# Second layer of a graph network: the running count of the placing scan moves into a PSUM bank, and its multiplication goes ahead of the next scan

## Chip, cores and metric

The kernel runs on one core of a Trainium2 chip (trn2). The metric is device time in microseconds (us) of one execution; the time of the kernel before is the median of three runs.

## What is computed

Two layers of a graph network over 12500 nodes of 128 channels and 400000 edges that are sorted by `dst`. The first is an attention layer over the edges. The second, which the change touches, is a weighted sum of neighbours, a linear layer and a normalization:

```python
x = _layernorm(x + _L0_gnn_ref(x, node_vec, edge_weight, edge_attr_64, edge_index, ...))
# second layer: rows = src, cols = dst, vals = edge_weight
gathered = vals[:, None] * x[cols]
agg = jax.ops.segment_sum(gathered, rows, num_segments=N_NODES)
x = _layernorm(x + jnp.einsum('nc,oc->no', agg, W) + b)
```

The edges are sorted by `dst`, but the second layer sums by `src`. So each edge's message must first be brought to a place beside the other messages of its target.

## The kernel before

**Blocks and steps.** The nodes are cut into 98 blocks of 128 (NB = 98). The second layer takes the edges in 808 steps of four tiles of 128 edges (G = 4, so 512 edges a step), in unrolled rounds of eight steps; in a round `st.k` runs from 0 to 7 and `st.i` counts the rounds. All engines run through the same steps, each with its stages at fixed leads: `(count_stage, 9)` in a step means that the count of the step nine ahead is done there. Each engine issues its stages in the order in which `body1` lists them, and semaphores tie the stages together.

**How an edge finds its place.** SyncE loads for each edge the number of its `src` block (`blk_row`, to 98 partitions). On VectorE `in_blk_stage` (L1751) compares it with the partition's number and so makes `in_blk`, 98 x 512 values of 0 or 1 in bf16, two buffers. `count_stage` (L1769) runs a scan along the 512 edges, state times one plus membership, so that each block's partition holds its running count; the scan starts from the last element of the former step's scan, or, in the first step of a round, from `carry`, which `carry_stage` (L1757) makes of that element and a jump from a table. The ones are read from bank 7 (`one_ps`). The scan writes `ranks`, which are the two halves of `y_all` in SBUF, taken in turn. `found_stage` (L1776) multiplies the ranks by the membership into one of four buffers `found1`, so that each edge keeps only the count of its own block. TensorE sums these over the partitions with a vector of ones (`rank_stage`, L1045), and VectorE copies the result to the table (`posw_stage`, L1783).

**The message.** VectorE makes a one-hot of the edges' `dst` (`onehot1_stage`, L1794), TensorE gathers with it the rows of the node matrix (L1063), ScalarE scales them into a ring of four steps (`rows_out`, L1261 and L1262) and takes the table rows (`take1`, L1254); VectorE forms the offsets (`rel_stage`, L1788) and the final index (`pick_stage`, L1801, and `place_stage`, L1808). GpSimd then issues four indirect scatters a step to DRAM (L869), after it has waited for the rows and for the index.

**Segments.** From round 26 of 101 on, a second stream runs in the same loop: SyncE loads messages back in their new order (three segments a step), VectorE makes their one-hots (`seg_rels`, L1821, and `seg_onehots`, L1828), TensorE multiplies (L1077), and VectorE adds the three products to the sums in SBUF (`seg_add`, L1838), each add waiting for the one before. After the pairs' last step the segments run alone, and the closing normalization follows.

**The waits around the change.** A scan waits for `s_inblk`, for `s_pos` up to the multiplication of the step two before it (two places), and for `s_carry`, which counts scans and carries. The multiplication waits for `s_carry` and for the rank matmul that last read its output buffer. `s_pos` counts the multiplications. Bank 0 is unused in this part of the kernel.

Of the kernel before, what the change touches and what calls it, by code (L numbers as in the profile page):

```python
# [19 lines left out]
ALU = mybir.AluOpType  # L20
# [3 lines left out]
P = 128  # L24
G = 4
# [24 lines left out]
def build(nc, x, src, dst, attr, weight, node_vec, time_w, time_b, Wq, bq, Wk, bk, Wv, bv, We, Wskip, bskip, W1, b1, out):  # L50
# [5 lines left out]
    NB = -(-N // P)  # L56
# [30 lines left out]
    with ctx:  # L87
        def sb(name, shape, dt=F32):
            return ctx.enter_context(nc.sbuf_tensor(name, shape, dt))

        def sem(name):
            return ctx.enter_context(nc.semaphore(name))
# [32 lines left out]
        jump = sb("jump", [P, NCHUNKS])  # L125
        carry = sb("carry", [P, 1])
# [56 lines left out]
        prod = y_all[:, :].rearrange("p (k e) -> p k e", k=2)  # L183
# [29 lines left out]
        def part(n):  # L213

            rest1[0] += n
            return kv_flat[:, rest1[0] - n:rest1[0]]
# [4 lines left out]
        in_blk = part(G * P).bitcast(BF16).rearrange("p (k e) -> p k e", k=2)  # L221
# [12 lines left out]
        seg_oh = oh_all[:, RING1 * G * P:RING1 * G * P + SEG_OH * SEGMENT * 2 * P].rearrange("p (h b a n) -> p h b a n", h=SEG_OH, b=SEGMENT, a=2)  # L234
        assert MT == 4 * SEGMENT and UNROLL1 % (MT // SEGMENT) == 0
        blk_row = feat_flat[:, RING1 * 2 * P:RING1 * 2 * P + KS * G * P // 2].bitcast(BF16).rearrange("p (k e) -> p k e", k=KS)
        ranks = prod
        found1 = [featT_all[:, 0, :], featT_all[:, 1, :], feat_flat[:, 0:G * P], feat_flat[:, G * P:2 * G * P]]
        zeros = oh_all[:, QS * G * P * 2 - (CHUNK * NCHUNKS - COLS) * 4:QS * G * P * 2]
        W7 = FB * C  # L240
# [32 lines left out]
        def hist(n, of):  # L273
# [26 lines left out]
        banks = [ctx.enter_context(nc.psum_tensor(f"bank{i}", [P, 512], F32)) for i in range(8)]  # L300
# [2 lines left out]
        featT_ps = banks[1][0:TD + MSG, :]  # L303
        e_ps, q_ps = banks[2:4], banks[4:6]
        agg_ps = [banks[6 + j][:, 0:HEADS * HB] for j in range(2)]
        irow_ps, one_ps = banks[7][:, 0:P], banks[7][0:NB, P:P + 1]
        RANKS = SEGMENT * P
        mT_ps, small_ps = banks[0][:, 0:G * ROWS], banks[0][:, 128:128 + 4 * ROWS]
# [35 lines left out]
        s_chunk, s_carry, s_inblk, s_rank, s_pos, s_posw = (sem(n) for n in (  # L344
            "s_chunk", "s_carry", "s_inblk", "s_rank", "s_pos", "s_posw"))
# [17 lines left out]
        def wait(eng, s, value):  # L363

            if not isinstance(value, int) or value > 0:
                eng.wait_ge(s, value)
# [26 lines left out]
        def Step1(i, k):  # L393
            return Step(i, k, UNROLL1)

        def exists(st, steps):
            return not isinstance(st.s, int) or 0 <= st.s < steps
# [54 lines left out]
        def at1(i, k, *stages):  # L452

            for stage_of, ahead in stages:
                st = Step1(i, k + ahead)
                if exists(st, STEPS1):
                    stage_of(st)

        def seg(i, k, b, ahead, pairs, stage_of):
            st = Step1(i, k + ahead)  # L460
            first, end = (BEGIN, LOOPS1) if pairs else (LOOPS1, ENDS)
            if not isinstance(st.s, int) or UNROLL1 * first <= st.s < UNROLL1 * end:
                stage_of(Segment(st, b))
# [829 lines left out]
        def _(dve):  # L1293
# [459 lines left out]
            def carry_stage(st):  # L1753

                if st.k == 0 and not (isinstance(st.i, int) and st.i == 0):
                    dve.wait_ge(s_carry, st.s + st.i - 1)
                    dve.tensor_tensor(carry[0:NB, :], ranks[0:NB, 1, G * P - 1:G * P], jump[0:NB, bass.ds(st.i, 1)], ALU.add).then_inc(s_carry, 1)  # L1757

            def count_stage(st):

                dve.wait_ge(s_inblk, st.s + 1)
                wait(dve, s_pos, st.before(2))
                first = isinstance(st.i, int) and st.i == 0
                if st.k == 0:
                    since = jump[0:NB, 0:1] if first else carry[0:NB, :]
                else:
                    since = ranks[0:NB, (st.k + 1) % 2, G * P - 1:G * P]
                wait(dve, s_carry, st.s + st.i)
                dve.tensor_tensor_scan(ranks[0:NB, st.k % 2, :], one_ps.to_broadcast([NB, G * P]), in_blk[0:NB, st.k % 2, :], since,  # L1769
                                       ALU.mult, ALU.add).then_inc(s_carry, 1)  # L1770

            def found_stage(st):

                dve.wait_ge(s_carry, st.s + st.i + 1)
                wait(dve, s_rank, st.before(4))
                dve.tensor_tensor(found1[st.k % 4][0:NB, :], ranks[0:NB, st.k % 2, :], in_blk[0:NB, st.k % 2, :], ALU.mult).then_inc(s_pos, 1)  # L1776

            def posw_stage(st):

# [32 lines left out]
            def seg_blocks(i, k):  # L1812
                sg = Segment(Step1(i, k), 0)
                seg_blk[k] = several(mybir.EngineType.DVE, seg_blk_i[0:1, bass.ds(sg.q, SEGMENT)], NB)
# [25 lines left out]
            def body1(i, pairs, segs):  # L1840
                for k in range(UNROLL1):
                    own = segs and (not isinstance(i, int) or i >= (BEGIN if pairs else LOOPS1))
                    if segs:
                        seg(i, k, 0, 2, pairs, seg_onehots)
                    if own:
                        seg_blocks(i, k)
                    if pairs:
                        at1(i, k, (onehot1_stage, 2), (carry_stage, 9), (count_stage, 9))
                    if segs:
                        seg(i, k, 0, 0, pairs, seg_add)  # L1850
                    if pairs:
                        at1(i, k, (posw_stage, 6), (place_stage, 0), (found_stage, 8))
                    if segs:
                        seg(i, k, 1, 0, pairs, seg_add)
                    if pairs:
                        at1(i, k, (rel_stage, 4), (in_blk_stage, 10))
                    if segs:
                        seg(i, k, 2, 0, pairs, seg_add)
                    if pairs:
                        at1(i, k, (pick_stage, 1))  # L1860
                    if segs:
                        seg(i, k, 0, 3, pairs, seg_rels)
# [13 lines left out]
            dve.wait_ge(s_base1, 1)  # L1876
            dve.wait_ge(s_acc1, 1)
            second(dve, body1)

            def products(g, i, k):  # L1880
# [63 lines left out]
```

## Time and profile before

| | |
|---|---|
| median of 3 runs | 9850.37 us (9843.33 to 9854.15) |
| the profiled execution | 9864.48 us |
| its span in the trace | 9862.8 us |
| VectorE busy | 8560.3 us (87%) |
| TensorE busy | 7624.6 us (77%) |
| GpSimd busy | 6708.6 us (68%) |
| ScalarE busy | 5115.0 us (52%) |
| TensorE's granted clock, mean | 0.822 |

The span is the time from the first to the last instruction of the profiled execution. DVE is VectorE, ACT is ScalarE, POOL is GpSimd, PE is TensorE and PEld its weight load, SP is SyncE. A busy share is an average over both layers; the second layer's pairs lie between 5225 and 9449 us. In a row of the timeline the number in brackets is the time for which the engine was idle ahead of the instruction, with what ended it.

### The profile page before, as it was taken

The numbers are of one execution on the slowest core, as the hardware profiler recorded it, in microseconds if no ns is written. First come the engines' busy times: TensorE is split into PE (matmuls) and PEld (weight loads), VectorE is DVE, ScalarE is ACT, GpSimd is POOL, SyncE is SP. The second block draws the span as 40 slices with busy tenths as digits, with TensorE's granted clock in tenths as the row PEclk, the third lists the DMA queues.
The fourth block names the chain that finished last, engine by engine and source line by source line (L and its number), as shares of the span: only waits on it lengthen the run. The fifth ranks groups of instructions, "written<-read, shape, count | busy, mean of one in ns | idle before, by whom it ended". The sixth has DMA issues, their size and how long they took to land.

```text
span 9862.8 us, 272152 instructions
## 1 busy us (share of the span) xinstructions
PE 7624.6 (77%) x52868; PEld 7101.3 (72%) x52869; DVE 8560.3 (87%) x21301; ACT 5115.0 (52%) x20838; POOL 6708.6 (68%) x6871
## 2 busy tenths in 40 slices
PE   6477777777777777777756777788888888888855
PEld 2477777777777777777756777787888877877754
DVE  5899999999999999999987666799999999999968
ACT  2377777777777777777753333333333333333300
POOL 0477777777777777777745777777777777777720
PEclk8688988888888888898875555688888888888888
DMA  6467666676666666666632222355555555555544
GB/s 191 114 180 178 179 177 177 178 179 178 176 177 180 177 176 177 178 181 177 177 97 69 71 71 71 106 151 147 149 147 149 148 148 149 148 148 149 148 133 116
DMA packets 1631706, 1484.67 MB, mean 151 GB/s; under 512 B 792007, under 2 KB 1363043, under 8 KB 1631203
## 3 DMA queue, kind: packets, MB, share of 16 engines
q1 hardware_dynamic: 1374244, 848.34, 34.3%
q0 software_dynamic: 257088, 632.95, 22.8%
q14 instruction: 335, 2.74, 0.1%
q8 instruction: 39, 0.64, 0.0%
HBM read 1225.51 MB, written 254.87 MB: 150 GB/s over the span
## 4 chain that ended last, share of the span: by engine, by line
issue 25%; DVE 19%; POOL 18%; PE 14%; DMA 7%; ACT 7%; DVEq 6%; SPq 3%; ACTq 2%; POOLq 0%
POOL message_scratch L869 17%; DMA message_scratch<-ohT,idx 6%; PE bank L982 3%; DVE y_all L1537 3%; PE bank L973 3%; ACT arena L1154 2%; DVEq L531 2%; PE bank L955 2%; PE bank L1015 2%; PE bank L963 2%; DVE acc L1670 1%; SPq L728 1%; DVE oh L1583 1%; DVE oh L1576 1%; DVE kve L1523 1%
## 5 line engine op out<-in xcount | busy, mean ns | idle before, releaser
L817 POOL DMA_INDIRECT kv<-kv_scratch,arena x3136 | 3265.7, 1041 | 1236.6 <-issue 837.5
L869 POOL DMA_INDIRECT message_scratch<-ohT,idx x3232 | 3214.2, 994 | 1079.0 <-issue 880.2
L1261 ACT ACTIVATE ohT<-bank,kv 128x128 f32<-128x128 f32 x3232 | 923.9, 369 | 2703.8 <-DMA message_scratch<-ohT,idx 2665.1
L1154 ACT ACTIVATE arena<-arena,weights 128x65 f32<-128x65 f32 x7040 | 1771.6, 337 | 2.4 <-PE bank L982 2.3
L1063 PE MATMUL bank<-acc,oh 128*128 x6464 | 1211.2, 345 | 520.3 <-ACT ohT L1262 514.4
L1063 PEld LDWEIGHTS bank<-acc,oh 128*128 128x128 f32 x6464 | 1054.7, 247 | 627.7 <-issue 625.2
L1077 PE MATMUL bank<-oh,kve 128*128 128x128 f32 x8640 | 1387.7, 321 | 144.7 <-DVE arena L1838 107.8
L982 PE MATMUL bank<-arena,oh 128*128 128x130 f32 x7040 | 1164.1, 318 | 280.8 <-DVE acc L1670 274.8
L1077 PEld LDWEIGHTS bank<-oh,kve 128*128 128x128 f32 x8640 | 1248.0, 227 | 167.8 <-issue 157.3
L982 PEld LDWEIGHTS bank<-arena,oh 128*128 128x128 f32 x7040 | 1048.2, 227 | 362.6 <-issue 295.1
L973 PE MATMUL bank<-arena,ohT 128*128 128x128 f32 x7040 | 1090.6, 306 | 0.0
L973 PEld LDWEIGHTS bank<-arena,ohT 128*128 128x128 f32 x7040 | 1031.3, 225 | 0.3 <-issue 0.2
L1161 ACT ACTIVATE featT<-bank 96x512 f32<-96x512 f32 x880 | 518.3, 589 | 917.0 <-PE bank L955 895.0
L963 PE MATMUL bank<-We,featT 96*128 96x128 f32 x7040 | 979.5, 284 | 18.3 <-ACT featT L1161 18.3
L963 PEld LDWEIGHTS bank<-We,featT 96*128 96x128 f32 x7040 | 914.3, 202 | 21.4 <-ACT featT L1161 20.1
L1178 ACT ACTIVATE feat<-wrow,rel 128x32 f32<-128x32 f32 x3520 | 830.6, 308 | 163.7 <-POOL rel L825 161.2
L1769 DVE TENSOR_TENSOR_SCAN y_all<-bank,y_all,kv 98x512 f32<-98x512 f32 x707 | 900.4, 1274 | 0.2
L955 PE MATMUL bank<-ident,feat 128*96 128x128 f32 x3520 | 610.7, 301 | 311.9 <-ACT feat L1167 297.5
L1828 DVE TENSOR_TENSOR oh<-bank,kv 128x768 f32<-128x768 f32 x720 | 689.5, 958 | 76.3 <-DVE kv L1821 37.5
L1518 DVE TENSOR_TENSOR arena<-kv,bank 128x512 f32<-128x512 f32 x880 | 597.9, 679 | 159.2 <-PE bank L963 103.6
L1045 PEld LDWEIGHTS bank<-ones,featT 98*128 98x128 f32 x3232 | 516.9, 242 | 226.6 <-issue 173.5
L1794 DVE TENSOR_SCALAR oh<-bank,icol 128x512 f32<-128x512 f32 x808 | 605.5, 749 | 74.5 <-issue 35.5
(232 smaller groups left out, 12653.6 us busy)
## 6 DMA issues: line engine op xcount, KB each, us to landing
kve<-message_scratch SPq DMA_DIRECT2D x2160, 129.0 KB
kve<-nodes_scratch SPq DMA_DIRECT2D x880, 256.0 KB
feat<-in_edge_attr_dram SPq DMA_DIRECT2D x880, 96.0 KB
feat<-block_scratch SPq DMA_DIRECT2D x812, 98.0 KB
arena<-q_scratch SPq DMA_DIRECT2D x880, 64.0 KB
message_scratch<-ohT,idx POOLq DMA_INDIRECT x3232
kv<-kv_scratch,arena POOLq DMA_INDIRECT x3136
feat<-in_edge_attr_dram SPq DMA_DIRECT2D x880, 32.0 KB
```

The lines of the kernel that those rows point to most:

```text
L817: pool.indirect_dma_start(kv[:, k, g, :], None, kv_d, bass.IndirectOffsetOnAxis(ap=group_rows[:, half, k * G + g, 0:1].bitcast(I32), axis= ...
L869: pool.indirect_dma_start(msg_d, bass.IndirectOffsetOnAxis(ap=idx[:, k, g:g + 1], axis=0), sum_ring[:, k % RING1, g, :], None).then_inc(s_ ...
L955: op = pe.transpose(featT_ps[:, g * P:(g + 1) * P], feat[:, k, g, :], ident[:, :])
L963: op = pe.matmul(e_ps[st.k % 2][:, g * P:(g + 1) * P], featT[:, st.k % 2, g * P:(g + 1) * P], We1[:, :], start=True, stop=True)
L973: op = pe.matmul(q_ps[st.k % 2][:, g * P:(g + 1) * P], ohT[:, r, g * P:(g + 1) * P], qb[:, r, :], start=True, stop=True)
L982: op = pe.matmul(agg_ps[st.k % 2], oh[:, st.k % QS, g, :], wv[:, st.k % 2, g, :, :].rearrange("p h c -> p (h c)"), start=(g == 0), stop=(g ...
L1063: op = pe.matmul(banks[2 + st.k % 2][:, g * P:(g + 1) * P], oht1[:, st.k % RING1, g * P:(g + 1) * P], acc[:, bass.ds(places[g], C)], start ...
L1077: op = pe.matmul(banks[4 + sg.half][:, b * P:(b + 1) * P], mt[:, sg.slot(MT) + b, a, 0:C], seg_oh[:, sg.half, b, a, :], start=(a == 0), st ...
L1154: op = act.activation(wv[:, st.k % 2, g, h, :], vR[:, st.k, g, h, :], ACT.Copy, scale=weights[:, st.k // ROUND, g, st.k % ROUND, h:h + 1])
L1178: op = act.activation(feat[:, k, g, 0:TD], wrow[:, :], ACT.Copy, scale=of[:, g:g + 1])
L1261: act.activation(sum_ring[:, st.k % RING1, g, 0:C], banks[2 + st.k % 2][:, g * P:(g + 1) * P], ACT.Copy, scale=taken[:, st.k, g, 2:3])
L1769: dve.tensor_tensor_scan(ranks[0:NB, st.k % 2, :], one_ps.to_broadcast([NB, G * P]), in_blk[0:NB, st.k % 2, :], since, ALU.mult, ALU.add). ...
```

## The change

`ranks` becomes one place of 98 x 512 values, all of bank 0 in PSUM, in place of the two halves of `y_all` in SBUF. The scan writes it there, and the multiplication, the carry and the next scan's start value read it there. As there is one place, a scan now waits for the multiplication of the step right before it (`wait(dve, s_pos, st.s)`). The multiplication's stage is moved: in a step of the loop it stood behind `place_stage`, between the first and the second add; now it stands behind `onehot1_stage` and ahead of the carry and the scan. Its lead of eight steps stays, and so do all other stages.

```diff
--- before.py
+++ after.py
@@ -234,7 +234,6 @@
         seg_oh = oh_all[:, RING1 * G * P:RING1 * G * P + SEG_OH * SEGMENT * 2 * P].rearrange("p (h b a n) -> p h b a n", h=SEG_OH, b=SEGMENT, a=2)
         assert MT == 4 * SEGMENT and UNROLL1 % (MT // SEGMENT) == 0
         blk_row = feat_flat[:, RING1 * 2 * P:RING1 * 2 * P + KS * G * P // 2].bitcast(BF16).rearrange("p (k e) -> p k e", k=KS)
-        ranks = prod
         found1 = [featT_all[:, 0, :], featT_all[:, 1, :], feat_flat[:, 0:G * P], feat_flat[:, G * P:2 * G * P]]
         zeros = oh_all[:, QS * G * P * 2 - (CHUNK * NCHUNKS - COLS) * 4:QS * G * P * 2]
         W7 = FB * C
@@ -303,6 +302,7 @@
         featT_ps = banks[1][0:TD + MSG, :]
         e_ps, q_ps = banks[2:4], banks[4:6]
         agg_ps = [banks[6 + j][:, 0:HEADS * HB] for j in range(2)]
+        ranks = banks[0][0:NB, :]
         irow_ps, one_ps = banks[7][:, 0:P], banks[7][0:NB, P:P + 1]
         RANKS = SEGMENT * P
         mT_ps, small_ps = banks[0][:, 0:G * ROWS], banks[0][:, 128:128 + 4 * ROWS]
@@ -1754,26 +1754,26 @@
 
                 if st.k == 0 and not (isinstance(st.i, int) and st.i == 0):
                     dve.wait_ge(s_carry, st.s + st.i - 1)
-                    dve.tensor_tensor(carry[0:NB, :], ranks[0:NB, 1, G * P - 1:G * P], jump[0:NB, bass.ds(st.i, 1)], ALU.add).then_inc(s_carry, 1)
+                    dve.tensor_tensor(carry[0:NB, :], ranks[:, G * P - 1:G * P], jump[0:NB, bass.ds(st.i, 1)], ALU.add).then_inc(s_carry, 1)
 
             def count_stage(st):
 
                 dve.wait_ge(s_inblk, st.s + 1)
-                wait(dve, s_pos, st.before(2))
+                wait(dve, s_pos, st.s)
                 first = isinstance(st.i, int) and st.i == 0
                 if st.k == 0:
                     since = jump[0:NB, 0:1] if first else carry[0:NB, :]
                 else:
-                    since = ranks[0:NB, (st.k + 1) % 2, G * P - 1:G * P]
+                    since = ranks[:, G * P - 1:G * P]
                 wait(dve, s_carry, st.s + st.i)
-                dve.tensor_tensor_scan(ranks[0:NB, st.k % 2, :], one_ps.to_broadcast([NB, G * P]), in_blk[0:NB, st.k % 2, :], since,
+                dve.tensor_tensor_scan(ranks, one_ps.to_broadcast([NB, G * P]), in_blk[0:NB, st.k % 2, :], since,
                                        ALU.mult, ALU.add).then_inc(s_carry, 1)
 
             def found_stage(st):
 
                 dve.wait_ge(s_carry, st.s + st.i + 1)
                 wait(dve, s_rank, st.before(4))
-                dve.tensor_tensor(found1[st.k % 4][0:NB, :], ranks[0:NB, st.k % 2, :], in_blk[0:NB, st.k % 2, :], ALU.mult).then_inc(s_pos, 1)
+                dve.tensor_tensor(found1[st.k % 4][0:NB, :], ranks, in_blk[0:NB, st.k % 2, :], ALU.mult).then_inc(s_pos, 1)
 
             def posw_stage(st):
 
@@ -1845,11 +1845,11 @@
                     if own:
                         seg_blocks(i, k)
                     if pairs:
-                        at1(i, k, (onehot1_stage, 2), (carry_stage, 9), (count_stage, 9))
+                        at1(i, k, (onehot1_stage, 2), (found_stage, 8), (carry_stage, 9), (count_stage, 9))
                     if segs:
                         seg(i, k, 0, 0, pairs, seg_add)
                     if pairs:
-                        at1(i, k, (posw_stage, 6), (place_stage, 0), (found_stage, 8))
+                        at1(i, k, (posw_stage, 6), (place_stage, 0))
                     if segs:
                         seg(i, k, 1, 0, pairs, seg_add)
                     if pairs:
```

## Rows read from the trace of the kernel before

**Rows 1.** The page, busy time of each engine over the span

```profile
PE 7624.6 (77%) x52868; PEld 7101.3 (72%) x52869; DVE 8560.3 (87%) x21301; ACT 5115.0 (52%) x20838; POOL 6708.6 (68%) x6871
```

**Rows 2.** The scatter's line: durations (min/median/max), releasers of its idle time

```profile
L869 POOL DMA_INDIRECT message_scratch<-ohT,idx x3232: 955/962/1526, 5250.1 to 9447.8; - x191
...
  issue: 880.2, 2889
```

**Rows 3.** Windows of the second layer: start:end, length, busy time (count), clock, DMA

```profile
5250.10:6339.70 1089.60, 847.33 (x4292) 795.94 (x4290) 677.12 (x1742) 381.36 (x2100) 836.15 (x832) 0.51 0.26 75
6339.70:9448.70 3109.00, 2602.40 (x18981) 2457.81 (x18980) 2846.64 (x7780) 1095.98 (x5947) 2378.04 (x2400) 0.85 0.55 147
...
9383.00:9449.00 66.00, 26.27 (x191) 24.07 (x190) 22.85 (x75) 15.91 (x77) 50.09 (x52) 0.74 0.26 77
```

**Rows 4.** Timeline, VectorE and GpSimd: start, us, instruction, [idle before]

```profile
5252.87 0.97 POOL L869 DMA_INDIRECT message_scratch<-ohT,idx  x1 [0.30 <-ACT ohT L1262]
...
8002.06 1.27 DVE L1769 TENSOR_TENSOR_SCAN y_all<-bank,y_all,kv 98x512 f32<-98x512 f32 x1
8002.18 0.97 POOL L869 DMA_INDIRECT message_scratch<-ohT,idx  x1 [0.30 <-issue]
...
8003.25 0.26 DVE L1838 TENSOR_TENSOR arena<-arena,bank 128x128 f32 x1
...
8003.50 0.15 DVE L1808 TENSOR_TENSOR idx<-kv 128x4 int32<-128x4 f32 x1
...
8003.57 0.68 DVE L1776 TENSOR_TENSOR featT<-y_all,kv 98x512 f32<-98x512 f32 x1
...
8004.17 0.28 DVE L1838 TENSOR_TENSOR arena<-arena,bank 128x128 f32 x1
...
8008.32 0.68 DVE L1776 TENSOR_TENSOR featT<-y_all,kv 98x512 f32<-98x512 f32 x1
...
8008.51 1.32 POOL L869 DMA_INDIRECT message_scratch<-ohT,idx  x1 [0.31 <-issue]
...
9385.60 1.11 POOL L869 DMA_INDIRECT message_scratch<-ohT,idx  x1 [0.30 <-ACT ohT L1262]
```

**Rows 5.** Timeline of VectorE: four of its carries (every eighth step)

```profile
6403.56 0.15 DVE L1757 TENSOR_TENSOR carry<-y_all,jump 98x1 f32<-98x1 f32 x1
...
6484.78 0.15 DVE L1757 TENSOR_TENSOR carry<-y_all,jump 98x1 f32<-98x1 f32 x1
...
6564.03 0.15 DVE L1757 TENSOR_TENSOR carry<-y_all,jump 98x1 f32<-98x1 f32 x1
...
9383.39 0.15 DVE L1757 TENSOR_TENSOR carry<-y_all,jump 98x1 f32<-98x1 f32 x1
```

**Rows 6.** VectorE's waits from 6600 to 9200 us: total us, times, longest

```profile
DVE kv L1788 <- ACT kv L1254: 65.1, 108, 1.6
```

**Rows 7.** Groups by line and shape, VectorE: count, busy us, mean ns, idle before

```profile
L1769 DVE TENSOR_TENSOR_SCAN y_all<-bank,y_all,kv 98x512 f32<-98x512 f32 x707 | 900.4, 1274 | 0.2
...
L1537 DVE TENSOR_TENSOR y_all<-kve,bank 128x512 f32<-128x512 f32 x880 | 590.5, 671 | 0.0
...
L1776 DVE TENSOR_TENSOR featT<-y_all,kv 98x512 f32<-98x512 f32 x404 | 276.5, 684 | 0.0
```

**Rows 8.** Timeline of VectorE ahead of the layer: a copy into a bank

```profile
5219.87 0.29 DVE L1865 COPY bank<-irow 128x128 f32<-128x128 f32 x1
```

**Rows 9.** Timeline of VectorE in a step with a carry

```profile
8016.49 0.17 DVE L1821 TENSOR_TENSOR kv<-kve,seg_base 128x6 f32<-128x6 f32 x1
8016.70 0.96 DVE L1828 TENSOR_TENSOR oh<-bank,kv 128x768 f32<-128x768 f32 x1
...
8018.34 0.15 DVE L1757 TENSOR_TENSOR carry<-y_all,jump 98x1 f32<-98x1 f32 x1
8018.62 1.28 DVE L1769 TENSOR_TENSOR_SCAN y_all<-bank,carry,kv 98x512 f32<-98x512 f32 x1
```

**Rows 10.** Timeline of VectorE where segments run alone: three adds

```profile
9481.27 1.15 DVE L1838 TENSOR_TENSOR arena<-arena,bank 128x128 f32 x3
```

## The prediction, made before the changed kernel was run

> **What bounds the kernel now.** I read the page first: over the whole span VectorE is the busiest engine and GpSimd stands well behind it [rows 1]. That average hides two layers, so I went to the one line that GpSimd has in the second layer, L869, the indirect scatter. Of its 3232 instructions nearly all are preceded by the same 0.3 us, put down to issue [rows 2]; followed one after another, no gap after the first is longer than 0.32 us. So from 5250.1 to 9448.7 us GpSimd never waits for anybody: its own instructions, 0.96 us each at best plus 0.305 us, are the second layer's length. The reader is to see there that an engine shown "77% busy" is the bound.
>
> The change lies wholly inside this layer, so I cut it where segments start beside pairs [rows 3]. Pairs alone: 208 steps of four scatters, 1089.6 / 208 = 5.24 us a step, one scatter 836.15 / 832 = 1.005 us. Pairs with segments: 600 steps, 3109 / 600 = 5.18 us, one scatter 2378.04 / 2400 = 0.991 us. The shortest is 0.955, the median 0.962 [rows 2]; at 0.958 each the two stretches hold 836.15 - 797.1 = 39 us and 2378.04 - 2299.2 = 79 us of stretched scatters.
>
> The timeline tells who stretches them [rows 4]. A scatter that begins inside the scan (8002.18) or ahead of the multiplication takes 0.96 or 0.97; one that begins at 8008.51, inside the multiplication L1776 that began at 8008.32, takes 1.32. Going through all of them in order of time, 448 begin during L1776 (the first at 5252.87, the last at 9385.60), and they hold 33 of the 39 us and 69 of the 79 us; the rest is spread, mostly over L1751. L1776 has both inputs in SBUF; the scan and the adds L1838, which have one input in a bank, stretch nothing.
>
> The Trainium skill, "SBUF — State Buffer", section "Who interferes with whom", says that a VectorE instruction with two SBUF inputs contends with a GpSimd instruction that reads SBUF, and that one with at most one SBUF input does not. By that rule, the trace agrees: 1.32 against 0.97 us.
>
> VectorE is nearly as long as GpSimd. In the stretch where it catches up after the segments start, two rounds of 8 steps run from the carry at 6484.78 to that at 6564.03: 79.25 / 16 = 4.95 us a step [rows 5]. From 6564.03 to the last carry it keeps GpSimd's pace, 2819.4 / 544 = 5.18, and the difference shows as waits of L1788 for ScalarE, which the scatters' landing drives [rows 6]: 65.1 us over some 502 steps, 0.13 each. Hence VectorE's free pace lies between 4.95 and 5.18 - 0.13 - 0.03 (the overlap lost at each stop) = 5.02. I take 4.97, nearer the pace it was seen to run.
>
> **The parts.** *Multiplication reads a bank.* Its stretching goes: at most 33 us in pairs alone, 69 us beside segments. Its own time goes from 684 ns to about 672, which L1537 takes with one bank input [rows 7].
>
> *Scan writes a bank.* No large write of that kind is there. The nearest is a copy of 128 columns to a bank, 0.29 us [rows 8]; at the 1.04 ns a column that (684 - 150) / 512 gives for L1776, 0.13 of it are columns and 0.16 fixed, as for a small operation in SBUF (0.15 to 0.16) [rows 4]. I take +0.01 us; bounds 0 and +0.06.
>
> *Order.* Before, the multiplication stood behind the placing (L1808) and took 0.60 us of the chain (8003.57 to 8004.17) [rows 4], since an independent instruction starts 0.08 us ahead of its forerunner's end. Now it stands behind L1794, and the next scan must wait until it has finished, because there is one place. For a wait on the instruction right ahead the trace has two prices [rows 9]: L1821 to L1828, 0.04 us after the end; carry to scan, 0.13 us after (8018.34 + 0.15, then 8018.62). The scan has three waits, as it had there, so I take 0.13. Cost in such a step: 0.67 + 0.13 in place of 0.60 = +0.20. Every eighth step the carry stands between, needs only the former scan, and pays its own 0.13 already: 0. Mean 0.18. Bounds: gap 0.04, +0.10; gap 0.20 (one more sequencer step in the row, an estimate from 0.04 to 0.13), +0.24.
>
> *What the multiplication leaves behind.* It also hid the wait of the second add for the first. Where adds stand alone, three last 1.15 us [rows 10]: pitch 0.43, so a dependent add starts 0.14 after the end of the one before. The first add takes 0.26, so the second can start 0.40 after it; behind the placing it would start at 0.25 + 0.07 = 0.32. Exposed: +0.08 a step. The third add stays covered by L1788 and L1751.
>
> Nothing is queued differently on GpSimd or SyncE; TensorE's rank matmuls get their input earlier. Behind the waiting scan on VectorE stand adds, ranks and placing; GpSimd needs the placing, with some 17 us in hand: at 9383.39 it has 52 scatters left [rows 3] where 36 are for steps not yet placed.
>
> VectorE's new pace: 4.97 + 0.18 + 0.08 + 0.01 = 5.24 us. GpSimd's would be 4 x 1.265 = 5.06. So GpSimd stops being the bound beside segments, and VectorE takes over, slower than the 5.18 of today.
>
> **The sum.** In pairs alone VectorE has over 2 us of idle time a step (677 of 1090 us busy) [rows 3], so all 33 us are gained. The carry at 6403.56 [rows 5] moves to 6370.6. From it to the last carry are 576 steps: at 5.24, 3018.2 us, to 9388.8. That iteration's placing ends 1.9 later, GpSimd starts 0.3 after, and its last 36 scatters take 36 x 1.265 = 45.5: end at 9436.5 against 9448.7, -12 us. It is less bad than 576 x (5.24 - 5.173) = 39 us lost against 33 gained, because GpSimd's 17 us in hand are used up. What follows (segments alone, closing) starts from that end and is unchanged. The profiled execution took 9864.5 us around a span of 9862.8; mine would take 9852. The median of the three runs is 9850.4, 14 below it; I forecast 9850.4 - 12 = 9838.
>
> Pace and result hang together tightly: 0.01 us of pace is 5.8 us; no change lies at 5.26, slower by 20 us (0.2%, what a measurement here can tell) at 5.295, faster by 20 us at 5.225.
>
> **Rivals.**
> 1. *Waits on the instruction ahead cost nothing to speak of* and VectorE stays at about 5.0. Then GpSimd bounds all along: 3232 x 1.265 plus the 16 us of stretching not from L1776 ends at 9355, -95 us, 9756. For it: VectorE waits today. Against: the gaps of 0.04 to 0.14 in three places. Chance 0.16.
>  The Trainium skill, "VectorE: DVE Perf Modes", section "The DRAIN you can't avoid", gives eight copies the same 13.88 us with a semaphore after each or only after the last, so a wait would be free; the rows speak against it here.
> 2. *Waits are cheap*, 0.04: pace 5.16, -58 us, 9792. Chance 0.13.
> 3. *The other side: the scan waits longer.* With a gap of 0.20 and a free pace of 5.00, the pace is 5.33: 6370.6 + 3070 + 47.7 = 9488.4, +40 us, 9890. It decides from 5.295 on. For it: the scan's carried-value wait takes a computed number, which the sequencer may only work out after the wait for the multiplication. Against: the carry's 0.13 has such waits too. Chance 0.20.
> 4. *The stretching does not go* (the multiplication's read of block membership is enough for it): no 33 us, VectorE's pace as forecast, +21 us, 9871. Against: one-SBUF-input instructions stretch nothing in [rows 4]. Chance 0.07.
>
> The forecast itself has 0.44, its own range -32 to +20 us. Faster by over 0.2%: rivals 1, 2 and a third of the forecast, 0.42. Slower: rivals 3, 4 in the main, 0.25. Same: 0.33. The range reaches from beyond rival 2 to rival 3: 9785 to 9890; rival 1 stays out.
>
> **What would show it.** Scatters beginning inside the multiplication take 0.96; pairs alone run at about 5.08 a step. Beside segments the steps take 5.2 to 5.3, L1788 no longer waits for ScalarE, and GpSimd waits over 0.3 us for the placing. The scan starts 0.13 us after the multiplication's end, the second add 0.40 after the first. I am wrong if GpSimd still has no gap in the last 500 steps (rival 1 or 2), or if the scan into the bank takes clearly over 1.29 us.

## The result: slower by 0.9%

The changed kernel takes 9939.9 us (median of 6 runs, 9929.84 to 9945.12) against 9851.7 us for the kernel before (6 runs): a ratio of 1.0090, 95% interval 1.0077 to 1.0103. The forecast was 9838 us, faster by 12 us, with a range from 9785 to 9890.

The page of the changed kernel, busy time, answers to [rows 1]; below it the groups of the scatter and of the scan (count, busy us, mean ns, idle time ahead and what ended it):

```profile
PE 7697.1 (77%) x52868; PEld 7228.3 (73%) x52869; DVE 8687.4 (87%) x21301; ACT 5107.7 (51%) x20838; POOL 6589.1 (66%) x6871
...
L869 POOL DMA_INDIRECT message_scratch<-ohT,idx x3232 | 3102.6, 960 | 1269.2 <-issue 1140.2
...
L1769 DVE TENSOR_TENSOR_SCAN bank<-bank,kv 98x512 f32<-98x512 f32 x707 | 916.3, 1296 | 131.6 <-DVE feat L1776 57.5
```

GpSimd is busy for 119.5 us less and the whole is longer: its scatters average 960 ns where they took 994, but the idle time ahead of them has grown from 1079 to 1269 us. Before, no gap between two scatters was longer than 0.32 us; now 494 are longer than 0.33 us, so GpSimd waits. The scan, which had an idle time of 0.2 us in all its executions together [rows 7], now stands still for 131.6 us.

The scatter's line in the changed kernel, as in [rows 2], then the layer's two stretches, as in [rows 3] (pairs alone, pairs with segments; cut at the changed kernel's own steps 0, 208 and 808):

```profile
L869 POOL DMA_INDIRECT message_scratch<-ohT,idx x3232: 952/958/1082, 5250.0 to 9526.2; - x191
...
  issue: 1140.2, 3123
```

```profile
5250.00:6301.50 1051.50, 839.96 (x4285) 794.17 (x4283) 694.40 (x1737) 383.33 (x2100) 797.82 (x832) 0.51 0.29 77
6301.50:9527.20 3225.70, 2684.53 (x18984) 2588.28 (x18984) 2958.53 (x7783) 1086.53 (x5947) 2304.75 (x2400) 0.82 0.55 142
```

The longest scatter is 1.08 us where it was 1.53. Pairs alone take 1051.5 us in place of 1089.6, 38 us less; the 600 steps beside segments take 3225.7 in place of 3109.0, 117 us more. The sum is +79 us, and the span grew by 77.7 us (9940.5 - 9862.8). The medians differ by 88, above all because the profiled execution of before lay 13 us above its median (that of the changed kernel lay 2 above).

VectorE sets the pace. Two of its carries, the same ones as the first and last of [rows 5]:

```profile
6368.89 0.15 DVE L1757 TENSOR_TENSOR carry<-bank,jump 98x1 f32<-98x1 f32 x1
...
9479.40 0.15 DVE L1757 TENSOR_TENSOR carry<-bank,jump 98x1 f32<-98x1 f32 x1
```

(9479.40 - 6368.89) / 576 = 5.40 us a step, against 5.17 before (cut in the same way) and 5.24 forecast. Its waits from 6600 to 9200 us no longer hold one of L1788 for ScalarE [rows 6]; VectorE now waits mostly for itself:

```profile
DVE bank L1769 <- DVE feat L1776: 36.0, 180, 0.2
DVE bank L1769 <- DVE featT L1776: 34.0, 170, 0.2
DVE oh L1828 <- DVE kv L1821: 27.4, 58, 0.5
```

One step of the changed kernel in the timeline, VectorE alone except for one scatter, answers to [rows 4]:

```profile
8006.00 0.68 DVE L1776 TENSOR_TENSOR feat<-bank,kv 98x512 f32<-98x512 f32 x1
8006.23 0.96 POOL L869 DMA_INDIRECT message_scratch<-ohT,idx  x1 [0.30 <-issue]
8006.88 1.30 DVE L1769 TENSOR_TENSOR_SCAN bank<-bank,kv 98x512 f32<-98x512 f32 x1 [0.20 <-DVE feat L1776]
...
8008.09 0.27 DVE L1838 TENSOR_TENSOR arena<-arena,bank 128x128 f32 x1
...
8008.35 0.15 DVE L1808 TENSOR_TENSOR idx<-kv 128x4 int32<-128x4 f32 x1
8008.51 0.29 DVE L1838 TENSOR_TENSOR arena<-arena,bank 128x128 f32 x1
8008.80 0.16 DVE L1788 TENSOR_TENSOR kv<-kv 128x4 bf16<-128x4 f32 x1
8009.03 0.35 DVE L1751 TENSOR_SCALAR kv<-feat,icol 98x512 bf16<-98x512 bf16 x1
```

A scatter that begins 0.23 us into the multiplication takes 0.96 us: the contention is gone. But the scan starts 0.20 us after the multiplication's end, where an instruction that waits for nothing near starts 0.08 us before it; and the second add starts 0.42 after the first, where it would start about 0.33 after it if it followed the placing at once. The two short instructions behind the second add start late as well, 0.29 and 0.23 us after their forerunners' starts; the section on the prediction comes back to them.

### The profile page after: what moved, and what is told of

Read it like the earlier page. It is cut to its first block and busy times, and to the rows that moved or that the text cites. A ratio compares the mean times of both kernels' runs of the same rounds, so it can differ in the third digit from the quotient of the medians.

```text
span 9940.5 us, 272152 instructions
## 1 busy us (share of the span) xinstructions
PE 7697.1 (77%) x52868; PEld 7228.3 (73%) x52869; DVE 8687.4 (87%) x21301; ACT 5107.7 (51%) x20838; POOL 6589.1 (66%) x6871
## 5 line engine op out<-in xcount | busy, mean ns | idle before, releaser
L869 POOL DMA_INDIRECT message_scratch<-ohT,idx x3232 | 3102.6, 960 | 1269.2 <-issue 1140.2
L1077 PE MATMUL bank<-oh,kve 128*128 128x128 f32 x8640 | 1476.7, 335 | 139.1 <-DVE arena L1838 107.4
L1077 PEld LDWEIGHTS bank<-oh,kve 128*128 128x128 f32 x8640 | 1334.8, 241 | 161.6 <-issue 150.5
L1769 DVE TENSOR_TENSOR_SCAN bank<-bank,kv 98x512 f32<-98x512 f32 x707 | 916.3, 1296 | 131.6 <-DVE feat L1776 57.5
L1045 PE MATMUL bank<-ones,featT 98*128 98x1 f32 x3232 | 524.1, 283 | 354.3 <-DVE arena L1838 262.7
L1045 PEld LDWEIGHTS bank<-ones,feat 98*128 98x128 f32 x3232 | 527.3, 247 | 295.0 <-issue 290.3
```

The lines of the kernel that those rows point to most:

```text
L869: pool.indirect_dma_start(msg_d, bass.IndirectOffsetOnAxis(ap=idx[:, k, g:g + 1], axis=0), sum_ring[:, k % RING1, g, :], None).then_inc(s_ ...
L1045: op = pe.matmul(banks[4 + st.k % 2][:, RANKS + g:RANKS + g + 1], found1[st.k % 4][0:NB, g * P:(g + 1) * P], ones[0:NB, 0:1], start=True, ...
L1077: op = pe.matmul(banks[4 + sg.half][:, b * P:(b + 1) * P], mt[:, sg.slot(MT) + b, a, 0:C], seg_oh[:, sg.half, b, a, :], start=(a == 0), st ...
L1769: dve.tensor_tensor_scan(ranks, one_ps.to_broadcast([NB, G * P]), in_blk[0:NB, st.k % 2, :], since, ALU.mult, ALU.add).then_inc(s_carry, 1)
```

## The experiments

Two theories. *Theory 1*: waits on VectorE that nothing covers any more (scan behind multiplication, second add behind first) cost the time, and the bank is a gain. *Theory 2*: the bank is what costs, by the scan's writes or by reads beside TensorE's. Ten more kernels were run. "Pace" is VectorE's, worked out from the carries as above; "scan idle" is the idle time ahead of the 707 scans that follow no carry, from their group; "scatter" is the mean of GpSimd's 3232.

| kernel | median us | ratio to before (95%) | pace | scan idle, us | scatter, ns |
|---|---|---|---|---|---|
| before | 9851.7 | 1 | 5.17 | 0.2 | 994 |
| changed | 9939.9 | 1.0090 (1.0077 to 1.0103) | 5.40 | 131.6 | 960 |
| lead of nine, bank | 9742.9 | 0.9895 (0.9878 to 0.9911) | 5.05 | 0.2 | 959 |
| lead of nine, SBUF | 9841.7 | 0.9993 (0.9984 to 1.0003) | 5.16 | 0.2 | 988 |
| one place, SBUF | 9966.9 | 1.0119 (1.0102 to 1.0136) | 5.38 | 131.8 | 993 |
| order alone, SBUF | 9850.2 | 1.0003 (0.9994 to 1.0013) | 5.20 | 0.0 | 976 |
| changed, scan's carry wait out | 9877.4 | 1.0031 (1.0018 to 1.0043) | 5.33 | 67.0 | 960 |
| the same, other wait first | 9900.6 | 1.0055 (1.0038 to 1.0072) | 5.34 | 94.3 | 960 |
| changed, one wait on the scan | 9843.8 | 0.9999 (0.9990 to 1.0009) | 5.25 | 25.2 | 959 |
| changed, cover for the second add | 9886.6 | 1.0042 (1.0027 to 1.0056) | 5.32 | 131.7 | 959 |
| both cures | 9797.1 | 0.9940 (0.9923 to 0.9956) | 5.17 | 25.2 | 958 |
| lead of nine, bank, fewer waits | 9754.7 | 0.9896 (0.9880 to 0.9913) | 5.07 | 0.6 | 963 |

Medians of different rows come from different chips; the ratios are taken on the same chip. The layer's first scatter starts between 5237 and 5248 us in these ten, and at 5250.0 in the changed kernel; why is open, and expectations reckoned from the changed kernel's time can be some us too high by it.

### The bank without the waits

The multiplication goes back to its old spot, but works on the scan of its own step, so that it is done long before the next scan:

```diff
-                        at1(i, k, (onehot1_stage, 2), (found_stage, 8), (carry_stage, 9), (count_stage, 9))
+                        at1(i, k, (onehot1_stage, 2), (carry_stage, 9), (count_stage, 9))
...
-                        at1(i, k, (posw_stage, 6), (place_stage, 0))
+                        at1(i, k, (posw_stage, 6), (place_stage, 0), (found_stage, 9))
```

> The bank stays (one place in bank 0), the multiplication goes back behind the placing, but with a lead of nine steps, so that it works on the scan of its own step and the next scan finds it long done. Theory 1 (the changed kernel lost its time by waits on VectorE that nothing covers: the scan behind the multiplication, 0.20 us, and the second add behind the first, 0.09 us): both waits go, VectorE's pace beside segments falls from 5.40 to about 5.05 us a step, scatters keep their 0.96 us, GpSimd is the bound again at 5.06 to 5.10: 9755 to 9790 us, faster than both kernels. Theory 2 (the bank itself costs the time: the scan writing to it, reads next to TensorE's work): the pace stays near 5.4 and the time near 9940.

9742.9 us, 1.05% faster than before and 2% faster than the changed kernel. Its scatter line and its two stretches:

```profile
L869 POOL DMA_INDIRECT message_scratch<-ohT,idx x3232: 954/958/1092, 5243.9 to 9329.0; - x191
```

```profile
5243.90:6295.20 1051.30, 844.08 (x4288) 794.18 (x4287) 685.59 (x1742) 383.19 (x2100) 797.57 (x833) 0.51 0.28 77
6295.20:9330.00 3034.80, 2602.63 (x18983) 2497.55 (x18982) 2851.14 (x7780) 1093.07 (x5947) 2303.14 (x2400) 0.83 0.55 151
```

1051.3 / 208 = 5.05 and 3034.8 / 600 = 5.06 us a step: the same pace with and without segments, which is four scatters and their gaps, 4 x (0.959 + 0.305), and no gap is longer than 0.33 us, so GpSimd bounds all along. Pairs alone are as long as in the changed kernel; the whole difference lies beside segments, 3034.8 against 3225.7. The bank is in both. Theory 2 falls.

The time came out below what the expectation gave (9755 to 9790): it took 5.06 to 5.10 us a step and the pace is 5.05, with next to nothing left of the stretching, and the layer began 6 us earlier.

### The same without the bank

```diff
-        ranks = banks[0][0:NB, :]
+        ranks = prod[0:NB, 0, :]
```

> The version with the lead of nine (multiplication of the same step's scan, behind the placing), but its one place in SBUF: nothing of the bank is left, and no new wait. If the bank's whole worth is that GpSimd's scatters are no longer held up by a multiplication with two SBUF inputs, the time is that of before, 9835 to 9865, with scatters of 0.99 to 1.005 us on average; if it lies in the lead or the waits, near the 9743 of the version in the bank.

9841.7 us, 0.9993 of before. Its stretches:

```profile
5248.40:6328.30 1079.90, 846.70 (x4292) 796.58 (x4291) 684.79 (x1742) 383.08 (x2100) 826.17 (x833) 0.51 0.28 75
6328.30:9427.30 3099.00, 2604.23 (x18979) 2468.56 (x18979) 2839.52 (x7780) 1092.98 (x5947) 2367.34 (x2400) 0.85 0.57 147
```

GpSimd's busy time is 826.17 + 2367.34 = 3193.5 us against 3100.7 with the bank: 93 us of stretched scatters, and the spans differ by 9839.9 - 9740.5 = 99 us. So the bank is worth some 95 us where GpSimd bounds. The lead of nine by itself changes nothing that can be told from the noise (0.9984 to 1.0003).

### One place in SBUF

The same edit made in the changed kernel.

> The changed kernel with the one place in SBUF (first half of y_all) in place of bank 0; order and waits as in the changed kernel. Theory 1: VectorE keeps the waits, pace 5.36 to 5.40 (the scan is 22 ns shorter), and scatters that begin inside the multiplication are stretched again, which costs 33 us where pairs run alone and nothing beside segments, where VectorE bounds: 9950 to 9975 us. Theory 2 (the bank costs the time): near the 9850 of before.

9966.9 us, inside what theory 1 gave, and 117 us from what theory 2 gave. Pairs alone, and one scan in its timeline:

```profile
5243.00:6338.00 1095.00, 847.21 (x4279) 796.31 (x4278) 692.58 (x1738) 381.48 (x2100) 841.29 (x832) 0.51 0.26 74
```

```profile
5802.32 0.69 DVE L1776 TENSOR_TENSOR feat<-y_all,kv 98x512 f32<-98x512 f32 x1
...
5803.21 1.28 DVE L1769 TENSOR_TENSOR_SCAN y_all<-bank,y_all,kv 98x512 f32<-98x512 f32 x1 [0.20 <-DVE feat L1776]
```

The 43 us that the bank gave to pairs alone are lost again (1095.0 against 1051.5), and the gap of 0.20 (5802.32 + 0.69, then 5803.21) stands there as in the changed kernel: it has nothing to do with where the ranks lie. VectorE's pace is 5.38 against 5.40: these 0.02 us a step are what the bank costs VectorE.

### The price of the wait

Three kernels keep order and bank and change only how the scan waits. First, its wait for `s_carry` is made only where a carry stands ahead (the multiplication just ahead has waited for the same value):

```diff
-                wait(dve, s_carry, st.s + st.i)
+                if st.k == 0:
+                    wait(dve, s_carry, st.s + st.i)
```

> The changed kernel without the scan's wait for s_carry in the seven steps of a round where no carry stands ahead of it; the multiplication right ahead has waited for the same value already. If the gap between multiplication and scan is made of sequencer steps that follow the wait for the multiplication, one step goes: gap 0.20 to 0.13 us, pace 5.40 - 7/8 x 0.07 = 5.34, 576 x 0.06 = 35 us less: 9905. If the gap is the engine's own latency, it stays 0.20 and the time 9940.

Then the two waits that are left change places (`s_pos` first):

> As the kernel without the scan's wait for s_carry in seven steps of eight, and the wait for the multiplication is put first, ahead of that for block membership, so that it rides on the scan itself. Sequencer steps as the cause: gap 0.20 to 0.04 us, pace 5.40 - 7/8 x 0.16 = 5.26, 576 x 0.14 = 81 us less: 9860. Engine latency as the cause: 9940.

Then the wait for membership is made ahead of the multiplication, so that one wait is left on the scan:

```diff
+            def member_stage(st):
+                dve.wait_ge(s_inblk, st.s + 1)
...
-                        at1(i, k, (onehot1_stage, 2), (found_stage, 8), (carry_stage, 9), (count_stage, 9))
+                        at1(i, k, (onehot1_stage, 2), (member_stage, 9), (found_stage, 8), (carry_stage, 9), (count_stage, 9))
```

> The changed kernel with the scan's wait for block membership moved ahead of the multiplication and its wait for s_carry left out where no carry stands ahead, so that the scan has one wait alone, for the multiplication. Sequencer steps behind a wait as the cause of the gap: it rides on the scan, gap 0.20 to 0.04 us, pace 5.40 - 7/8 x 0.16 = 5.26, 576 x 0.14 = 81 us less: 9860. If the data need longer than that from multiplication to scan: gap 0.10 or more and 9900.

The scan's group in the three, in this order (kernel by kernel):

```profile
L1770 DVE TENSOR_TENSOR_SCAN bank<-bank,kv 98x512 f32<-98x512 f32 x707 | 916.4, 1296 | 67.0
```

```profile
L1770 DVE TENSOR_TENSOR_SCAN bank<-bank,kv 98x512 f32<-98x512 f32 x707 | 916.4, 1296 | 94.3 <-DVE feat L1777 18.6
```

```profile
L1769 DVE TENSOR_TENSOR_SCAN bank<-bank,kv 98x512 f32<-98x512 f32 x707 | 915.8, 1295 | 25.2
```

The gap ahead of a scan is on average 131.6 / 707 = 0.19 us with all waits, 0.09 with two, 0.13 with the two in the other order, 0.04 with one. The instructions and the data are the same in all four; so the gap is made by the sequencer, which does what stands between the wait for the multiplication and the scan only after this wait. The first kernel's gap fell to 0.09, further than the 0.13 expected, and its 9877.4 us is 28 below the expected 9905, of which 13 are the layer's earlier start (5237.4 us). The second kernel missed: the wait put first did not ride on the scan, and its gap is longer than with the old order. VectorE's sequencer computes a register there:

```profile
L1762 DVEq ALU_OP  x776: 40/40/45, 5270.3 to 9433.6; - x194
```

The wait rides on this computation and not on the scan: ahead of 679 of the 707 scans it starts 0.04 us after the multiplication's end, inside the gap. In 606 the scan starts 0.08 us behind the computation's start. In 71 others the gap is 0.25 (18.6 us of the idle time), though the computation starts as early; why stays open.

The third runs at 5.25 a step, as expected to 0.01, and its 9843.8 us is better than the expected 9860.

### The second add's cover

```diff
-                        at1(i, k, (posw_stage, 6), (place_stage, 0))
+                        at1(i, k, (posw_stage, 6), (place_stage, 0), (rel_stage, 4))
...
-                        at1(i, k, (rel_stage, 4), (in_blk_stage, 10))
+                        at1(i, k, (in_blk_stage, 10))
```

> The changed kernel with rel_stage (0.16 us) moved from behind the second add to between the placing and the second add, as cover for its wait. If the add's wait for the first add is exposed by 0.09 us, some 0.07 us a step come back: pace 5.33, 576 x 0.07 = 40 us less, 9900. If the add is not waiting for the first add, 9940.

```profile
8008.34 0.27 DVE L1838 TENSOR_TENSOR arena<-arena,bank 128x128 f32 x1
...
8008.66 0.15 DVE L1788 TENSOR_TENSOR kv<-kv 128x4 bf16<-128x4 f32 x1
8008.76 0.29 DVE L1838 TENSOR_TENSOR arena<-arena,bank 128x128 f32 x1
```

The second add still starts 0.42 after the first: it is held by the first, whatever stands between. L1788 now runs inside this time, and the pace falls from 5.40 to 5.32 (5.33 expected), 9886.6 us (9900 expected, 7 of the 13 by the layer's earlier start). With the single wait on the scan beside it:

> The changed kernel with both cures at once: one wait on the scan (5.25 us a step when alone, from 5.40) and rel_stage between the placing and the second add (5.32 when alone). If the two exposed waits are separate terms of VectorE's pace, they add: 5.40 - 0.15 - 0.08 = 5.17, and the time is 9844 - 576 x 0.08 = 9798. If they overlap, near 9840.

9797.1 us, pace (9328.03 - 6352.16) / 576 = 5.17. The two waits are separate terms.

### The order by itself

The kernel before with the multiplication moved ahead of the scan, and nothing else (ranks in two places, the old wait):

> The kernel before with the new order alone: the multiplication ahead of carry and scan, ranks still in two places of SBUF, the scan waiting only for the multiplication two steps back. If the order costs just the second add's exposed wait (0.09 us) and some 0.04 us of later starts, VectorE's free pace is 5.02 + 0.13 = 5.15 us, still under GpSimd's 5.18: 9830 to 9865, as before. If the order itself were what slows, 9900 or more.

9850.2 us, no change. But VectorE's pace is 5.20, not the 5.15 expected: the order alone already takes all that VectorE had in hand, and GpSimd begins to wait: 82 of its gaps are longer than 0.33 us, and its two stretches show 60 us less of busy time (3154.3 against 3214.2) at nearly the same length.

```profile
5247.90:6333.30 1085.40, 845.86 (x4285) 796.97 (x4284) 675.81 (x1734) 382.56 (x2100) 831.82 (x833) 0.51 0.27 75
6333.30:9439.80 3106.50, 2628.46 (x18984) 2532.47 (x18984) 2940.04 (x7786) 1083.74 (x5947) 2322.43 (x2400) 0.82 0.56 147
```

### Fewer waits where GpSimd bounds

The version with bank and lead of nine, with the scan's carry wait out in seven steps of eight and `s_pos` first.

> The version in the bank with the lead of nine, whose scan also drops the wait for s_carry in seven steps of eight. GpSimd bounds that version (no gap between scatters above 0.33 us), so less work of VectorE's sequencer should change nothing: 9735 to 9750. If VectorE still held it up somewhere: 9720 or less.

Its 9754.7 us lies 5 above what was expected, but its ratio is 0.9896, that of the version without this edit 0.9895 (its median was measured on a chip on which before took 9858.0). VectorE's waits are worth nothing there.

## Why the prediction was wrong

**Bound and contention: right.** GpSimd bound the layer before, and the stretching came above all from the multiplication's two SBUF inputs; pairs alone gained 38 us (33 forecast), and the carry that was to move to 6370.6 lies at 6368.89. By the rule of the Trainium skill, "SBUF — State Buffer", section "Who interferes with whom", this was to be expected, and the pair of lead-of-nine kernels, 93 us of GpSimd's time apart, agrees.

**VectorE takes over beside segments: right**, and so is the way from there to the end: from the last carry to the last scatter's end it is 9527.2 - 9479.4 = 47.8 us, forecast 47.7. GpSimd's steps in hand were used up as said.

**VectorE's new pace: the step that failed.** Forecast 5.24, measured 5.40, and 576 x 0.16 = 92 us is the whole miss (-12 forecast, +78 in the profiled executions). Two things failed in it: the scan's gap was taken from the wrong instruction, and what the multiplication covered for the short instructions behind it was put at nothing. The terms of that sum, one by one:

- *"The scan has three waits, as it had there, so I take 0.13"*: it is 0.20 in six of eight steps and 0.13 in one. The gap of 0.13 was read from the scan behind a carry [rows 9]; in the six, one more sequencer step stands between. With the mean gap of 0.19 the cost of a step is 0.68 + 0.19 - 0.60 = 0.27, times 7/8 = 0.24 in place of 0.18: +0.06. I had the 0.20 as a bound and gave rival 3 a fifth.
- *What the multiplication leaves behind*: the sum has the second add alone, and for the short instructions behind it nothing at all. From start to start, L1788 comes 0.227 us after the second add, L1751 0.114 after L1788 and L1821 0.136 after L1801 in the changed kernel (means of the last 72 rounds), 0.477 together. In the two free rounds of the kernel before, from 6484.78 on, they came after 0.198, 0.075 and 0.101, 0.374 together: +0.10.
- *"I take 4.97, nearer the pace it was seen to run"*: without the other terms 4.95 is left of the 5.40, the pace of those two rounds, so this step held: -0.02. (Inside it, single waits on VectorE differ by up to 0.03 each way and cancel.)
- *Scan into a bank*, +0.01: the scan takes 1296 ns in place of 1274 and the add behind it 273 in place of 261, but from start to start this is 0.02, as in the pair of kernels with one place (5.38 and 5.40): +0.01.
- *Second add exposed*, +0.08: it starts 0.42 after the first in place of 0.33: 0.09, so +0.01. Covering it was worth 0.08, part of which may be the gap ahead of L1788, which moved too.

Together +0.06 + 0.10 - 0.02 + 0.01 + 0.01 = 0.16.

The +0.10 arises in the same steps of every round. The step shown above from 8006.00 is one of them; the same step in a free round of the kernel before:

```profile
6521.74 0.28 DVE L1838 TENSOR_TENSOR arena<-arena,bank 128x128 f32 x1
6521.94 0.15 DVE L1788 TENSOR_TENSOR kv<-kv 128x4 bf16<-128x4 f32 x1
6522.02 0.35 DVE L1751 TENSOR_SCALAR kv<-feat,icol 98x512 bf16<-98x512 bf16 x1
```

L1788 and L1751 come here 0.20 and 0.08 us after their forerunners, in the changed kernel 0.29 and 0.23. In the changed kernel the sequencer's register computations for L1751 run from 8008.82 to 8008.98, and L1751 starts 0.05 later; before they ran from 6521.54 to 6521.70, while the multiplication was still busy. So the long multiplication also covered work of the sequencer for the short instructions behind it. Two experiments bear this out: with the order alone the three are 0.460 together, with the multiplication back behind the placing (lead of nine, bank) they are 0.373 again. No experiment shortened that work by itself.

The terms' bounds, all taken at their bad end, give 5.02 + 0.24 + 0.06 + 0.08 = 5.40 and +80 us; a range that had them together would have held the result. That would have been luck in part, since two of these bounds were too wide (the bank's 0.06, the free pace's 5.02) and stood in for the term that was missing.

**Rivals.** Rival 3, the longer wait of the scan, is what happened, for the reason it named (a computed number worked out after the wait) and with twice its price (+78 us against +40), since the short instructions came on top. Rival 2's gap of 0.04 was made by the kernel with one wait on the scan, and there the pace is 5.25, not rival 2's 5.16, again 0.09 too much. Rival 1, waits that cost nothing, does not hold for this chain of dependent instructions: they start 0.04 to 0.20 us after the end, an independent one 0.08 before it. The Trainium skill, "VectorE: DVE Perf Modes", section "The DRAIN you can't avoid", found with eight copies that a semaphore after each costs nothing extra; here the measurement decides, and waits do cost time. Rival 4 fell with the scatters of 0.96 us. (The chance of being faster by over 0.2%, put at 0.42, is 0.16 + 0.13 + 0.15 = 0.44 by its own terms; slower by over 0.2%, which is what came, had 0.25.)

## What to carry to other kernels

When a change relieves the engine that bounds, work out the pace of the next one to a hundredth, and add up the adverse bounds as well as the middle values. When a long instruction moves, ask what it covered where it stood: not only the wait of the next dependent instruction, but also the sequencer's work for the short ones behind it. An instruction that must wait for the one right ahead should have its wait alone, as the last thing before it; every other wait or register computation between them was paid here with 0.07 to 0.10 us. Better still, give the chain other instructions in between: here the same single place in the bank, with the multiplication behind the placing at a lead of nine, turned 0.9% slower into 1.05% faster than before.

## What the runs showed of the hardware

- A dependent VectorE instruction started 0.04, 0.09, 0.13 or 0.20 us after its forerunner's end, by what its sequencer had to do in between, with the same two instructions on the same data; an independent one starts 0.08 us before it. In 707 scans that is the difference between 25 and 132 us of idle time.
- VectorE's sequencer works ahead while a long instruction runs: register computations of 6521.54 to 6521.70 lay inside a multiplication of 0.68 us. Where the multiplication was moved away, the instruction that needs them came 0.15 us later (0.23 against 0.08 us after the one ahead, from start to start).
- A scatter of GpSimd is held up by a multiplication with two SBUF inputs if it begins inside it; with one input in a bank the longest of 3232 scatters is 1.08 to 1.10 us, with both in SBUF it is 1.49 to 1.53.
- A scan of 512 columns takes 1273 to 1282 ns into SBUF and 1296 into a bank; in the versions with a lead of nine the same scan into the bank averages 1285 to 1286.
